# Feed-forward stage: in each step TensorE issues the up-products of a batch ahead of the down-products of the batch preceding it

## What is computed

```python
h2 = _ln(x, norm_mlp_w, norm_mlp_b)
x = x + (jax.nn.gelu(h2 @ mlp_w1.T + mlp_b1, approximate=False) @ mlp_w2.T + mlp_b2)
...
h = h + x      # written to the output
```

## Time and profile before

| | us |
|---|---|
| median of 3 runs | 1693.22 (1692.04 to 1693.26) |
| the profiled execution, its own time | 1697.35 |
| its span, first to last instruction | 1695.5 |
| TensorE busy (matmuls), of the span | 1521.0 (90%) |
| VectorE busy | 1242.6 (73%) |
| ScalarE busy | 1102.5 (65%) |
| GpSimd busy | 1018.9 (60%) |
| mean granted TensorE clock | 0.938 |

### The profile page before, as it was taken

The page is one execution under the profiler, slowest core; times in us unless marked ns, Lnnn a source line. Parts: engine busy times, 40 slices in busy tenths (PEclk is TensorE's granted clock), DMA queues, the critical chain, the costliest instruction groups (busy, mean ns, idle before and its releaser), DMA issues. The chain is left out here.

```text
span 1695.5 us, 37358 instructions
## 1 busy us (share of the span) xinstructions
PE 1521.0 (90%) x8662; PEld 660.5 (39%) x8662; DVE 1242.6 (73%) x3454; ACT 1102.5 (65%) x2137; POOL 1018.9 (60%) x1375
## 2 busy tenths in 40 slices
PE   2767975889999999999999999999999999875998
PEld 0215962233333333333333333333333333212665
DVE  4995866478787878878787887878788887353442
ACT  1432770647878777787877878787777878823333
POOL 6841435466685677767567677757767775423443
PEclk9767986879999999999999999999999999957999
DMA  1321117365454565456456546546645643020221
GB/s 41 77 54 31 45 32 108 50 81 72 70 83 67 70 75 84 62 74 81 61 75 77 77 60 83 75 60 81 77 72 65 85 63 55 10 30 29 62 67 56
DMA packets 134645, 109.27 MB, mean 64 GB/s; under 512 B 24128, under 2 KB 127552, under 8 KB 134592
## 3 DMA queue, kind: packets, MB, share of 16 engines
q1 hardware_dynamic: 132544, 104.45, 41.9%
q0 software_dynamic: 2048, 4.20, 1.0%
HBM read 19.26 MB, written 8.39 MB: 16 GB/s over the span
## 5 line engine op out<-in xcount | busy, mean ns | idle before, releaser
L1122 ACT ACTIVATE probs<-psum 128x512 f32<-128x512 f32 (+3 forms) x1536 | 757.9, 550 | 256.2 <-PE psum L1237 247.4
L1022 DVE TENSOR_REDUCE mx_S<-psum 128x1 f32<-128x512 f32 x512 | 324.7, 679 | 50.3 <-PE psum L1217 50.0
L1022 DVE TENSOR_REDUCE mx_C<-psum 128x1 f32<-128x512 f32 x512 | 316.3, 676 | 32.0 <-PE psum L1217 32.0
L1018 DVE CUSTOM_DVE_ANT_0 psum<-psum,causal 128x128 f32<-128x128 f32 (+3 forms) x512 | 241.4, 515 | 95.3 <-PE psum L1217 94.2
L1217 PE MATMUL psum<-ks_S,qs_S 96*128 96x512 bf16 x512 | 197.0, 395 | 17.9 <-DVE mx_S L1022 8.7
L1217 PE MATMUL psum<-ks_C,qs_C 96*128 96x512 bf16 x512 | 199.8, 398 | 12.2 <-DVE mx_C L1022 9.5
L1237 PE MATMUL psum<-qs_C,ks_C 99*128 99x512 bf16 x512 | 188.6, 387 | 3.3 <-ACT probs L1122 2.9
L1237 PE MATMUL psum<-qs_S,ks_S 99*128 99x512 bf16 x512 | 188.0, 384 | 0.2 <-ACT probs L1122 0.2
L903 POOL CAST parts_q<-f_q 128x512 bf16<-128x512 f32 x48 | 29.2, 609 | 251.1 <-ACT f_q L1113 250.6
L1217 PE MATMUL psum<-ks_T,qs_T 96*128 96x128 bf16 (+3 forms) x512 | 157.4, 310 | 5.1 <-DVE mx_T L1018 3.7
L1237 PE MATMUL psum<-qs_T,ks_T 99*128 99x256 bf16 (+3 forms) x512 | 152.3, 302 | 1.8 <-ACT probs L1122 1.7
(11 more groups left out here) (182 smaller groups left out, 2720.1 us busy)
## 6 DMA issues: line engine op xcount, KB each, us to landing
qs_S<-parts_q SPq DMA_DIRECT2D x96, 128.0 KB, 4.4
ks_S<-parts_k SPq DMA_DIRECT2D x96, 128.0 KB, 4.8
qs_T<-parts_q SPq DMA_DIRECT2D x96, 128.0 KB, 4.5
ks_T<-parts_k SPq DMA_DIRECT2D x96, 128.0 KB, 4.6
qs_C<-parts_q SPq DMA_DIRECT2D x96, 128.0 KB, 4.4
ks_C<-parts_k SPq DMA_DIRECT2D x96, 128.0 KB, 4.8
w_in_S<-in_s_in SPq DMA_DIRECT2D x16, 257.0 KB, 2.8
w_in_T<-in_t_in SPq DMA_DIRECT2D x16, 257.0 KB, 2.7
```

The source lines that it names most:

```text
L1018: nc.vector.tensor_tensor_reduce(tile[:, 0:last_key], tile[:, 0:last_key], causal[:, T - last_key:T], 1.0, NEG, ALU.add, ALU.max, mx[kind] ...
L1022: nc.vector.tensor_reduce(mx[kind][:, n:n + 1], tile, AX_X, ALU.max, negate=True).then_inc(reduced, 1)
L1122: nc.scalar.activation(probs[:, group_place(kind, b, n // 4), n % 4, t0:T], psum[:, LOGITS + ring_place(kind, b, n, RC), t0:T], ACT.Exp, s ...
```

## The change

In TensorE's step the two parts are exchanged. The turn stays first. Everything else of the kernel, all waits and their values included, is as before.

```diff
@@ feed_forward, TensorE @@
                 def stages(b, odd):
                     if exists(b):
                         turn(b, odd)
+                    if exists(b - 2):
+                        up(b - 2, odd)
                     if exists(b - 3):
                         down(b - 3, 1 - odd)
-                    if exists(b - 2):
-                        up(b - 2, odd)
 
                 halves_of_pairs(pe, stages, 3, B // 2, B // 2 + 2)
```

## The result

| us | before | changed |
|---|---|---|
| median | 1693.24 (1692.04 to 1693.40) | 1716.38 (1715.55 to 1717.38) |
| span of the profiled execution | 1695.5 | 1713.8 |
| its own time | 1697.35 | 1715.58 |
| from the turn of step 3 to the end of the last down-products | 125.9 | 148.1 |

The changed kernel takes 1.0141 times as long (95% interval 1.0129 to 1.0153), 23.1 us more. The forecast was 1717.1. The spans of the two profiled executions differ by only 18.3 us, since the stages ahead of this one happened to be about 4 us shorter in the second: the same turn starts at 1562.21 in it and at 1566.12 in the earlier trace rows. The stage by itself grew by 22.2 us.

The account below looks back on a forecast made before the run. The prediction took a chain of up-products, last GELU and down-products, about 8.09 us a step, to bound the stage. Work and pauses 18.8 plus clock falls 5.1 made 23.9 us, moving the median from 1693.22 to 1717.1; range 1709 to 1724.

Parts of the forecast that it names:

- The dependence: On VectorE, `normalise` of the next batch is queued behind `finish`, which waits for down-products; TensorE's up-products covered both before.
- The size of the pause: TensorE's turn waits for `finish` and `normalise` on VectorE: 25.8 us over twelve turns, batches 4 to 15.
- The work of a step: On TensorE, from a turn's start to the end of the down-products: 0.49 + 3.44 + 3.84 = 7.77 us.
- the sum: Feed-forward stage from step 3's turn to the last down-products: work and pauses cost 18.8 us, 23.9 with clock falls.
- Rival 3: `xs` is ready when down-products end, so TensorE bounds: step 7.60 us in place of 8.09, 1684.2 us; 4%.
- The clock: TensorE's granted clock falls to half after three of the twelve pauses, 1.7 us each, 5.1 us together.
- rival 1: The pause before TensorE's turn comes but the clock stays: 1693.22 + 18.8 = 1712.0 us; 24%.
- Rival 2: TensorE's clock falls at nearly every one of twelve pauses: 20.4 us more, 1732.4 us; 7%.
- The ends: Steps 16 to 18, without turn or pause, take 17.9 us; the last three steps give 6 us back.

## Why the prediction was right

**The dependence.** All of it rested on reading that `normalise` of the next batch stands behind `finish` on VectorE, and that the up-products were what covered the two. Both edits that break this (the turn moved, or `normalise` moved) take the pause away (all but 0.37 us at batch 15 in the first). This is shown. In the kernel before, the second edit does nothing; the first was not tried there.

**The size of the pause.** Predicted 25.8 us over twelve turns, from VectorE's rows of the kernel before; the trace of after has 26.0 in twelve waits, in the groups that were read: three of 1.8 to 1.9 us, three of 2.2 to 2.3, five of 2.0, and 3.78 us at batch 15. Reading the pause from work that was already done, under cover, gave it within 1%.

**The work of a step.** This term was a little off. I took 7.77 us from a turn's start to the end of the down-products, with 3.84 for the latter, about what the chain of the earlier trace rows has (3.83). Behind up-products they take 3.73 (1623.79 to 1627.52): the sum should have had 7.66. That is 1.4 us over thirteen steps, and 0.3 in the last three; it is why the stage without its falls grew by 17.2 us (22.2 less 5.0 for the three), where the sum said 18.8. Rival 3 was priced too slow in a like way: the two kernels in which TensorE is the bound came to 12 us under the kernel before, where I had priced 9.0. Their step is 0.44 + 3.44 + 3.57 = 7.45 us, for the turn, the up-products and the down-products, and not 7.60.

**The clock.** I chose three falls of 1.7 us; the profiled execution has three, and they cost 1.6 to 1.7 us each (from the turn at 1629.76 to the next down-products 5.54 us in place of 3.93, for one). The number was a choice between bounds and hit by luck as much as by reasoning; the timed executions, 1715.55 to 1717.38, may not all have had three. What stood on rows was the price of one and that pauses of 2 us suffice: rival 1 (no falls, 1712.0) is out by the traces. The kernel with the pauses filled, at 1711.4, comes near it, with one fall left. Two readings there were loose. The new pause is five times the 0.42 us gap, not six. And the stage of before does have longer gaps: 0.78 us in each of the last three steps without a fall, and 2.28 and 2.65 us ahead of the turns of batches 1 and 2, where the clock was still at 0.50 (it rose at 1565.3), so that they tell nothing about a fall. Rival 2 (a fall at nearly every pause) did not come, but a pause 1 us longer brings it: 11 of 12.

**The ends.** Steps 16 to 18 gave back what was forecast: from the down-products' end of step 15, 1692.72, to the last, 1710.31, it is 17.6 us, predicted 17.9.

So the sum was 1.7 us above the growth of the stage in the profiled execution (23.9 against 22.2), and 0.8 us above that of the medians (23.9 against 23.1).

## What to carry to other kernels

When two blocks of work on one engine are exchanged, look at what the block that came last used to cover on the other engines, and not only at what the block that now comes first waits for; the length of the new pause stands in the trace of before, as the time that the other engines need from the end of the one to the start of the next. The idea of the change was sound (the down-products no longer wait for the GELU), and it paid 12 us as soon as the turn, or `xs`, had its cover back. A fast engine's queue should not hold work that is ready behind work that waits for the critical engine.

## What the runs showed of the hardware

Pauses of TensorE between 1.8 and 2.3 us, one in each step of some 9.8 us, were followed by a fall from 2.4 to 1.2 GHz two times in eleven in the changed kernel (a third fall followed the pause of 3.8 us) and three times in twelve where `base` was held back. Pauses of 2.8 to 3.1 us were followed by one ten times in eleven, and nine of these stretches at half clock were twice as long, 6.8 us. When needless transposes filled all but 0.2 to 0.4 us of such pauses, there was none, and none in the two kernels without pauses. The Trainium skill (TensorE: Matmul & The Clock Gate, HAM oscillation) asks for longer idle gaps than those of 1.8 to 3.1 us; here the measurement decides against it. What tells a pause with a fall from one of the same length without is not shown.

Four VectorE operations of 128x128 that took 1.11 us took 3.0 to 3.1 beside two GpSimd operations of 1.18 and 1.27 us, in eight of the ten kernels, and 1.11 at batch 15 once GpSimd was held back. GpSimd's operations were not slower for it. The Trainium skill (SBUF — State Buffer, Who interferes with whom) says that VectorE in a two-port mode and GpSimd exclude each other at the ports that they share. The traces agree, at 1.9 to 2.0 us for each meeting.
